# A graph attention layer on one core: edge features loaded a second time in transposed layout, in place of transposes on TensorE and copies on ACT

## The chip, the core and the metric

The kernel runs on one core of one Trainium2 chip. The metric is device time in microseconds (us) of the whole execution; lower is better. A core has TensorE (PE in the profile, with its weight loads as PEld), VectorE (DVE), ScalarE (ACT), GpSimd (POOL) and SyncE (SP), which only issues transfers here. The engines run side by side and wait for each other by semaphores.

## What is computed

One layer of graph attention over 6250 nodes and 206250 edges sorted by target node, then a residual addition. Cut to what matters:

```
h  = relu(layernorm(x))                       # (6250, 256)
xm = h @ W_n2m.T;  xl = xm @ Wl.T + bl;  xr = xm @ Wr.T + br       # (6250, 128)
e  = (edge_attr @ W_r2m.T) @ We.T             # (edges, 128), edge_attr is (206250, 32)
z  = xl[src] + xr[dst] + e
logits = sum over each head's 16 columns of leaky_relu(z, 0.2) * att       # 8 heads
alpha  = softmax of logits over the edges of each dst (own loop edge with the mean attributes added)
out    = segment_sum(xl[src] * alpha, dst) + bias
result = x + out @ W_m2n.T
```

## The kernel before

**Prologue.** The node tables are made: `xl_table` in DRAM (the rows that edges gather), `xr_parts` in SBUF (xr in three bfloat16 parts), `Wc` (the product of the two edge weights; its 32 rows stand four times over the 128 partitions) and `Wc2`, in which each pair of row groups is kept apart from the other by zeros. The list of edges is cut into pieces of 256 edges, and each piece is bound to a window of 128 target nodes.

**Edge loop.** 427 steps (`STEPS`), each of 512 edges: two pieces, h = 0 and 1. Every engine has its own stream of instructions, written by hand, in loops of 48 steps (`UNROLL`); `sweep` gives the step k and its place s in the loop. What an engine does in step k, in this order:

- SP (L748 to L770): for each piece a transfer of edge attributes into `rbf` (a ring of 24 steps, a partition holds two neighbouring edges of each piece), one of the one-hot's slots into `slot_bc` (a ring of 8), and the masks of the running maxima. Ahead of `rbf` it waits until ACT has copied the attributes of step k - 24 (`attr_ready`), ahead of `slot_bc` until VectorE has made the one-hot of step k - 8 (`ohT_ready`). At 16 steps in all it copies a part of x to the output.
- GpSimd (L773 to L780): four gathers of 128 rows each of `xl_table` into `xl_g` (a ring of 24). It waits only for `msg_ready` of step k - 24.
- TensorE: z, transposed (128 features by 256 edges in each of two banks), is summed from three products of `xr_parts` with the one-hot (L794), the edge product `Wc2` by `rbfT` (L800: four matmuls of 128 columns, of which the two pieces use rows 0 to 63 and 64 to 127 of the array), and `xl_g` turned by the identity (L813). Between these last two stands the transpose of the next step's `rbf` (L808) into bank 2. Then come the logits of step k - 1 (L844) and the aggregation of step k - 17 (`LAG`, L860), whose first half's sum, `U_ps[0]`, lies in bank 2 too.
- ACT: distances and one-hots for the aggregation (L898, L903), the copy of the transposed attributes into `rbfT` (L907), the relu of z (L913), and the copy of `rbf` into `msg` (L915).
- VectorE: the addition of the first half's sum to `acc` (L955), the one-hot of step k + 2 (L965), the second half's addition (L979), the messages of step k - 16 (L989, L993), and `uT` of step k (L999), after which z's banks are free for the next step (`u_ready`).

Every 8 steps (`BATCH`) the running maxima of the softmax are brought up to date (L1008 and behind, L825, L833, L870).

**Finale.** Seven batches of node windows: loop edges, shares, projection, addition of x.

Of the kernel before, what the change touches and what calls it, by code (L numbers as in the profile page):

```python
# [36 lines left out]
SRING = 8  # L37
MRING = 3
# [77 lines left out]
def gat_kernel(nc, x, src, dst, edge_attr, W_n2m, W_r2m, Wl, bl, Wr, br, We, att, bias, W_m2n, out):  # L116
# [10 lines left out]
    with ExitStack() as ctx:  # L127
        def sb(name, shape, dt=FP32):
# [11 lines left out]
        Wc2 = sb("Wc2", [P, PT, D_MSG])  # L140
# [6 lines left out]

        banks = ctx.enter_context(nc.psum_tensor("banks", [P, 8, 512], FP32))
# [3 lines left out]
                 xr_parts, ident, ident16, ones, iota_n, node_of, att_bc, att_pad, Wc, Wc2, W_outT,  # L152
                 bias_col, minus_slot, src_tab, win_tab, edge_tab)

        acc = sb("acc", [P, WINDOWS, AGG])
        edge_loop(nc, banks, xl_table, slot_dram, masks_dram, edge_attr,
                  xr_parts, ident, ident16, ones, iota_n, node_of, att_pad, Wc2, minus_slot, src_tab, win_tab,
# [4 lines left out]
def prologue(nc, banks, xl_table, meta_dram, slot_dram, masks_dram, inputs,  # L162
             xr_parts, ident, ident16, ones, iota_n, node_of, att_bc, att_pad, Wc, Wc2, W_outT,
             bias_col, minus_slot, src_tab, win_tab, edge_tab):
# [5 lines left out]
    with ExitStack() as ctx:  # L170
# [3 lines left out]
        def sem(name):  # L174
# [58 lines left out]
        rows_in = [sem(f"rows_in{i}") for i in range(CHUNKS)]  # L233
# [6 lines left out]
        halo_set, head_set, pad_set, att_placed, w2_set, w2_ready = map(  # L240
            sem, ("halo_set", "head_set", "pad_set", "att_placed", "w2_set", "w2_ready"))
# [290 lines left out]
        def _(dve):  # L532
# [118 lines left out]
def edge_loop(nc, banks, xl_table, slot_dram, masks_dram, edge_attr,  # L651
              xr_parts, ident, ident16, ones, iota_n, node_of, att_pad, Wc2, minus_slot, src_tab, win_tab, edge_tab,
# [10 lines left out]
    with ExitStack() as ctx:  # L663
# [11 lines left out]
        rbfT = sb("rbfT", [P, 2, P])  # L675
# [21 lines left out]
        rbfT_ps, LT_ps = banks[:, 2, 0:P], [banks[:, 3 + 3 * par, 0:PIECE] for par in (0, 1)]  # L697
# [679 lines left out]
```

## Time and profile before

| | |
|---|---|
| Time, median of 3 runs | 3654.3 us (3628.19 to 3661.28) |
| Span of the profiled execution, first to last instruction | 2427.2 us |
| Granted TensorE clock, mean | 0.984 |
| Data moved | 244.85 MB, mean 101 GB/s |
| Edge loop in the span | from about 127 to 2337 us |

The profile tells of one execution, from its first to its last instruction. The times come from the whole execution; for the profiled one no total is given beside its span, and what fills the difference to the runs' times isn't in the profile. A row "x1708 | 1637.8, 959 | 522.9 <-issue 515.0" reads: 1708 instructions, engine busy 1637.8 us with them, 959 ns for one, and the engine idle for 522.9 us just before them, 515.0 of it ended by nothing that the profile shows. Matmuls overlap, so the start of the next block tells more than the length of one. An fp32 matmul is recorded as two instructions.

### The profile page before, as it was taken

The page shows a single profiled execution, that of the slowest core. Times are in us where ns is not written, and L with a number is a line of the kernel's source. Part 1 is how long each engine was busy: PE and PEld are TensorE (multiplying, and loading weights), DVE is VectorE, ACT ScalarE, POOL GpSimd, SP SyncE. Part 2 cuts the span into 40 slices and gives each one's busy share as a digit, 9 for nine tenths or more (in the row PEclk, how much of TensorE's full clock was granted, in tenths as well). Part 3 has the DMA queues.
Part 4 walks back from the last instruction along what each step waited for, and adds up shares of the span by engine and source line. Part 5 has one row for each costly group of instructions (what it writes and reads, how often), then busy time and mean ns, then how long its engine had stood idle before and what let it go on. Part 6 is the DMA issues. An engine that isn't in the chain of part 4 may idle for free. (4 is left out here: it accounts for less than half of the span.)

```text
span 2427.2 us, 71208 instructions
## 1 busy us (share of the span) xinstructions
PE 2249.0 (93%) x16556; PEld 1730.1 (71%) x16557; DVE 1481.8 (61%) x4178; ACT 1438.7 (59%) x4332; POOL 1722.3 (71%) x1914
## 2 busy tenths in 40 slices
PE   3968999989999999999999999999999999999977
PEld 2745777767777777777777777777777777777756
DVE  4734656656666666566656665666566656666677
ACT  2714666656665666566656665666566656666653
POOL 3777777777777777777777777777777777777501
PEclk9989999999999999999999999999999999999999
DMA  6244444444444444444444444444444444444117
GB/s 199 80 110 94 103 103 98 97 101 105 99 100 101 106 98 98 101 107 98 98 101 106 98 99 102 106 99 99 101 105 98 99 102 106 98 99 99 47 45 130
DMA packets 288536, 244.85 MB, mean 101 GB/s; under 512 B 168519, under 2 KB 259624, under 8 KB 287842
## 3 DMA queue, kind: packets, MB, share of 16 engines
q1 hardware_dynamic: 221742, 116.00, 21.3%
q0 software_dynamic: 60704, 120.20, 21.2%
q10 hardware_dynamic: 5652, 3.68, 0.5%
q8 instruction: 169, 2.77, 0.5%
q14 instruction: 269, 2.20, 0.3%
HBM read 228.23 MB, written 19.40 MB: 102 GB/s over the span
## 5 line engine op out<-in xcount | busy, mean ns | idle before, releaser
L778 POOL DMA_INDIRECT xl_g<-xl_table,src_tab x1708 | 1637.8, 959 | 522.9 <-issue 515.0
L999 DVE SCALAR_TENSOR_TENSOR uT<-banks,relu 128x256 f32<-128x256 f32 x854 | 347.3, 422 | 544.4 <-issue 517.8
L860 PE MATMUL banks<-msg,onehot 128*128 128x177 f32 x3416 | 632.3, 328 | 7.0 <-DVE acc L955 2.6
L860 PEld LDWEIGHTS banks<-msg,onehot 128*128 128x128 f32 x3416 | 516.8, 191 | 168.8 <-issue 152.3
L898 ACT ACTIVATE distance<-iota_n,minus_slot 128x128 f32<-128x128 f32 x1708 | 541.1, 390 | 0.0
L813 PE MATMUL banks<-ident,xl_g 128*128 128x128 f32 x3416 | 464.2, 280 | 36.2 <-DMA xl_g<-xl_table,src_tab 35.8
L813 PEld LDWEIGHTS banks<-ident,xl_g 128*128 128x128 f32 x3416 | 443.5, 201 | 44.5 <-DMA xl_g<-xl_table,src_tab 43.8
L913 ACT ACTIVATE relu<-banks 128x256 f32<-128x256 f32 x854 | 315.9, 383 | 149.6 <-PE banks L813 116.0
L794 PE MATMUL banks<-onehotT,xr_parts 128*128 128x256 bf16 x2562 | 356.4, 276 | 23.8 <-issue 18.6
L903 ACT ACTIVATE onehot<-distance 128x512 f32<-128x512 f32 x427 | 269.0, 630 | 113.9 <-PE banks L860 101.4
L907 ACT ACTIVATE rbfT<-banks 128x128 f32<-128x128 f32 x427 | 116.5, 273 | 353.5 <-PE banks L808 342.1
L955 DVE TENSOR_TENSOR acc<-acc,banks 128x177 f32 x427 | 145.0, 340 | 285.4 <-PE banks L860 212.3
L800 PE MATMUL banks<-rbfT,Wc 64*128 64x128 f32 x3416 | 310.1, 301 | 0.0
L794 PEld LDWEIGHTS banks<-onehotT,xr_parts 128*128 x2562 | 245.8, 98 | 76.8 <-issue 34.1
L989 DVE TENSOR_TENSOR msg<-xl_g,banks 128x512 f32<-128x512 f32 x427 | 291.1, 682 | 2.8 <-PE banks L871 2.4
L800 PEld LDWEIGHTS banks<-rbfT,Wc 64*128 64x128 f32 x3416 | 227.5, 189 | 90.3 <-issue 88.9
L844 PE MATMUL banks<-uT,att_pad 128*64 128x256 f32 x1708 | 280.8, 408 | 0.0
L808 PE MATMUL banks<-ident,rbf 128*128 128x128 f32 x427 | 141.7, 332 | 42.6 <-DVE acc L955 33.6
L965 DVE TENSOR_SCALAR onehotT<-slot_bc,node_of 128x512 bf16<-128x512 bf16 x427 | 153.1, 359 | 9.9 <-DMA slot_bc<-slot_dram 8.8
L979 DVE TENSOR_TENSOR acc<-acc,banks 128x177 f32 x427 | 144.3, 338 | 12.8 <-PE banks L860 4.9
L844 PEld LDWEIGHTS banks<-uT,att_pad 128*64 128x64 f32 x1708 | 85.1, 136 | 66.0 <-DVE uT L999 25.4
L808 PEld LDWEIGHTS banks<-ident,rbf 128*128 128x128 f32 x427 | 59.7, 140 | 101.5 <-DVE acc L955 46.8
(200 smaller groups left out, 1642.2 us busy)
## 6 DMA issues: line engine op xcount, KB each, us to landing
slot_bc<-slot_dram SPq DMA_DIRECT2D x427, 128.0 KB
xl_g<-xl_table,src_tab POOLq DMA_INDIRECT x1708
rbf<-in_edge_attr SPq DMA_DIRECT2D x854, 32.0 KB
masks<-masks_dram SPq DMA_DIRECT2D x864, 12.1 KB
out<-in_x SPq DMA_DIRECT2D x16, 336.0 KB
out<-result POOLq DMA_DIRECT2D x6, 896.0 KB, 9.5
xl_table<-lr_sb SPq DMA_DIRECT2D x49, 64.0 KB, 1.5
xl_in<-xl_table SPq DMA_DIRECT2D x7, 448.0 KB, 4.7
```

The costliest lines, as they stand in the source:

```text
L778: pool.indirect_dma_start(out=xl_g[:, k % RING, t], out_offset=None, in_=xl_table, in_offset=bass.IndirectOffsetOnAxis(ap=src_tab[:, e:e + ...
L794: nc.tensor.matmul(z_ps[h], parts_of(xr_parts, w[h], part), onehotT[:, n4, h * PIECE:(h + 1) * PIECE], start=part == 0, stop=False)
L800: nc.tensor.matmul(z_ps[h][:, i::PT], Wc2[q, i], rbfT[q, n], start=False, stop=False)
L808: nc.tensor.transpose(rbfT_ps, rbf[:, n], ident[:]).then_inc(rbfT_done, 1)
L813: mm = nc.tensor.matmul(z_ps[h][:, i::PT], xl_g[:, s % RING, i * SPLIT + h], ident[:], start=False, stop=i == PT - 1)
L844: mm = nc.tensor.matmul(LT_ps[par][h * ROWS:(h + 1) * ROWS], att_pad[:, ROWS - HEADS - i * HEADS:2 * ROWS - HEADS - i * HEADS], uT[:, n, h ...
L860: mm = nc.tensor.matmul(U_ps[h], onehot[:, j % 2, t], msg[:, j % 2, t], start=i == 0, stop=i == PT - 1)
L898: nc.scalar.activation(distance[:, t], iota_n[:], ACT.Abs, bias=minus_slot[:, one(TILES * (k - LAG + 1) + t)]).then_inc(dist_ready, 1)
L903: nc.scalar.activation(onehot[:, m % 2], distance[:], ACT.Relu, scale=-1.0, bias=1.0).then_inc(oh_ready, TICK)
L913: nc.scalar.activation(relu[:, h], z_ps[h], ACT.Relu, scale=1.0 - SLOPE).then_inc(relu_ready, 2 + h)
L989: nc.vector.tensor_tensor(to[:, :, :, 0:D_HEAD], xl_g[:, m % RING].rearrange("p t (h d) -> p t h d", d=D_HEAD), w_ps[:, :, row].unsqueeze( ...
L999: nc.vector.scalar_tensor_tensor(out=uT[:, s % 2, h * PIECE:(h + 1) * PIECE], in0=z_ps[h], scalar=SLOPE, in1=relu[:, h], op0=ALU.mult, op1 ...
```

## The change

The host passes a second array, `attr_cols`, which is `edge_attr_32` transposed (32 rows of 206250). SP loads for each piece of a step 32 rows by 256 edges of it into `attrT`, a ring of 4 steps (`TRING`): piece 0 lies in partitions 0 to 31, piece 1 in 32 to 63. TensorE multiplies `Wc` by it with two matmuls of 256 columns. The transposes, bank 2's part for them, ACT's copies, `rbfT` and `Wc2` with its fill and copies go. `rbf` is still loaded, for the copy into `msg`, ahead of which ACT now waits for its transfer. Ahead of a step's first transfer SP waits until TensorE has finished z of step k - 4.

```
@@ edge_loop, sync
-                    for h, e in enumerate(entries(nc, mybir.EngineType.SP, edge_tab, k, E - PIECE)):
+                    edges = entries(nc, mybir.EngineType.SP, edge_tab, k, E - PIECE)
+                    if inside(k - TRING, STEPS):
+                        sp.wait_ge(z_done, Z * (k - TRING + 1))
+                        sp.sem_inc(z_seen, 1)
+                    for h, e in enumerate(edges):
+                        sp.dma_start(attrT[h * D_RBF:(h + 1) * D_RBF, s % TRING], attr_cols[:, bass.DynSlice(e, PIECE)]
+                                     ).then_inc(turned_in[s % TRING], 16)
                         sp.dma_start(rbf[:, s % RING, h * PT * D_RBF:(h + 1) * PT * D_RBF],
...
@@ edge_loop, tensor
-                    pe.wait_ge(rbfT_ready, k + 1)
-                    for i in range(PT):
-                        for h in range(SPLIT):
-                            q = slice(h * PT * D_RBF, (h + 1) * PT * D_RBF)
-                            nc.tensor.matmul(z_ps[h][:, i::PT], Wc2[q, i], rbfT[q, n], start=False, stop=False)
-                if inside(k + 1, STEPS):
-                    n = (s + 1) % RING
-                    pe.wait_ge(loads[n], (r * (UNROLL // RING) + (s + 1) // RING + 1) * FULL)
-                    if inside(k, STEPS):
-                        pe.wait_ge(rbfT_ready, k + 1)
-                    if inside(k - LAG - 1, STEPS):
-                        pe.wait_ge(added, TICK * (k - LAG - 1) + 1)
-                    nc.tensor.transpose(rbfT_ps, rbf[:, n], ident[:]).then_inc(rbfT_done, 1)
-                if inside(k, STEPS):
+                    pe.wait_ge(turned_in[s % TRING], (r * (UNROLL // TRING) + s // TRING + 1) * FULL)
+                    for h in range(SPLIT):
+                        q = slice(h * D_RBF, (h + 1) * D_RBF)
+                        nc.tensor.matmul(z_ps[h], Wc[q], attrT[q, s % TRING], start=False, stop=False)
...
-                        if h == 0 and inside(k + 1, STEPS):
-                            pe.wait_ge(rbfT_ready, k + 2)
@@ edge_loop, scalar
-                if inside(k + 1, STEPS):
-                    act.wait_ge(rbfT_done, k + 2)
-                    nc.scalar.activation(rbfT[:, (s + 1) % 2], rbfT_ps, ACT.Copy).then_inc(rbfT_ready, 1)
...
+                    act.wait_ge(loads[m % RING], (r * (UNROLL // RING) + (s - LAG + 1) // RING + 1) * FULL)
@@ prologue, vector
-            nc.vector.memset(Wc2[:], 0.0).then_inc(w2_set, 1)
-            dve.wait_ge(w2_set, 1)
-            for t in range(TILES):
-                q = slice(t * D_RBF, (t + 1) * D_RBF)
-                nc.vector.tensor_copy(Wc2[q, t % PT], Wc[q, :]).then_inc(w2_ready, 1)
@@ kernel
-        a = np.ascontiguousarray(inputs[name])
+        arrays[f"in_{name}"] = np.ascontiguousarray(inputs[name])
+        if name == "edge_attr_32":
+            arrays["in_attr_cols"] = np.ascontiguousarray(np.asarray(inputs[name]).T)
```

How it stands on TensorE, from the edge product of a step inside the loop to its aggregation, before:

```order
L800 MATMUL banks<-rbfT,Wc 128x128 [waits rbfT_ready]
L800 MATMUL banks<-rbfT,Wc 128x128 x3
L808 MATMUL banks<-ident,rbf 128x128 [waits added,rbfT_ready,loads5]
L813 MATMUL banks<-ident,xl_g 128x128 [waits gathers4]
L813 MATMUL banks<-ident,xl_g 128x128 x3
L844 MATMUL banks<-uT,att_pad 64x256 [waits u_ready]
L844 MATMUL banks<-uT,att_pad 64x256
L860 MATMUL banks<-msg,onehot 128x177 [waits added,oh_ready,rbfT_ready,attr_ready,msg_ready]
```

The same place in the changed kernel, where the lines are L801 (edge product), L805 (xl_g), L825 (a batch's work, which falls on this step), L836 (logits) and L850 (aggregation):

```order
L801 MATMUL banks<-attrT,Wc 128x256 [waits turned_in1]
L801 MATMUL banks<-attrT,Wc 128x256
L805 MATMUL banks<-ident,xl_g 128x128 [waits gathers5]
L805 MATMUL banks<-ident,xl_g 128x128 x3
L825 MATMUL banks<-ones,end_row 128x1 [waits lr_ready]
L825 MATMUL banks<-ones,end_row 128x1
L836 MATMUL banks<-uT,att_pad 64x256 [waits u_ready]
L836 MATMUL banks<-uT,att_pad 64x256
L850 MATMUL banks<-msg,onehot 128x177 [waits oh_ready,added,attr_ready,msg_ready]
```

Two matmuls stand in place of four, the transpose and its waits are gone, and the wait for the attributes is now one for a transfer.

On SP, one step inside the loop, before (L87 reads the pieces' first edges from a table):

```order
L87 ISA [waits attr_ready]
L87 TENSOR_LOAD edge_tab
L752 ISA
L752 DMA rbf<-in_edge_attr 128x64
L752 ISA
L752 DMA rbf<-in_edge_attr 128x64
L756 REGISTER_ALU
L757 ISA [waits ohT_ready]
L757 DMA slot_bc<-slot_dram 128x512
```

And the same step of the changed kernel:

```order
L88 ISA [waits attr_ready]
L88 TENSOR_LOAD edge_tab
L749 ISA
L752 REGISTER_ALU [waits z_done]
L752 DMA attrT<-in_attr_cols 32x256
L754 ISA
L754 DMA rbf<-in_edge_attr 128x64
L752 REGISTER_ALU
L752 DMA attrT<-in_attr_cols 32x256
L754 ISA
L754 DMA rbf<-in_edge_attr 128x64
L758 REGISTER_ALU
```

The transfer of `slot_bc` follows behind these rows as before; ahead of it there are now four transfers in place of two, and the wait for `z_done`.

## Rows read from the trace of the kernel before

**Rows 1.** The page: busy time by engine; SP's DMA queue (packets, MB, share).
```profile
PE 2249.0 (93%) x16556; PEld 1730.1 (71%) x16557; DVE 1481.8 (61%) x4178; ACT 1438.7 (59%) x4332; POOL 1722.3 (71%) x1914
...
q1 hardware_dynamic: 221742, 116.00, 21.3%
```

**Rows 2.** Groups of instructions: the gathers.
```profile
L778 POOL DMA_INDIRECT xl_g<-xl_table,src_tab x1708 | 1637.8, 959 | 522.9 <-issue 515.0 <-DVE msg L989 5.2 <-DVE msg L993 2.7
```

**Rows 3.** The gathers' line: ns min/median/max, first and last start.
```profile
L778 POOL DMA_INDIRECT xl_g<-xl_table,src_tab x1708: 940/944/1910, 127.7 to 2285.0; - x190
```

**Rows 4.** TensorE in order of time, a short step (start us, us).
```profile
1207.14 0.82 PE L794 MATMUL banks<-onehotT,xr_parts 128*128 128x256 bf16 x6
1207.88 0.72 PE L800 MATMUL banks<-rbfT,Wc 64*128 64x128 f32 x8
1208.53 0.33 PE L808 MATMUL banks<-ident,rbf 128*128 128x128 f32 x1
1208.70 1.10 PE L813 MATMUL banks<-ident,xl_g 128*128 128x128 f32 x8
1209.72 0.65 PE L844 MATMUL banks<-uT,att_pad 128*64 128x256 f32 x4
1210.31 1.47 PE L860 MATMUL banks<-msg,onehot 128*128 128x177 f32 x8
1211.61 0.82 PE L794 MATMUL banks<-onehotT,xr_parts 128*128 128x256 bf16 x6
```

**Rows 5.** Who waited for whom: us in total, times, longest us.
```profile
ACT rbfT L907 <- PE banks L808: 342.1, 318, 9.8
...
PEld banks L813 <- DMA xl_g<-xl_table,src_tab: 43.8, 40, 2.9
...
PEld banks L860 <- ACT rbfT L907: 14.2, 37, 0.4
...
DVE onehotT L965 <- DMA slot_bc<-slot_dram: 8.8, 4, 4.3
```

**Rows 6.** The same view of SP's queue.
```profile
SPq L87 <- ACT msg L915: 497.3, 340, 14.6
```

**Rows 7.** TensorE in order of time at the loop's end.
```profile
2288.03 1.16 PE L813 MATMUL banks<-ident,xl_g 128*128 128x128 f32 x8
```

**Rows 8.** The transposes' line: what ended TensorE's idle time before them.
```profile
  DVE acc L955: 80.3, 128
```

**Rows 9.** Prologue in order of time: copies of Wc2, first projection.
```profile
62.43 0.96 DVE L618 COPY Wc<-Wc 32x128 f32<-32x128 f32 x4
...
66.14 0.42 DVE L634 TENSOR_TENSOR lr_sb<-banks,lr_bias 128x256 f32<-128x256 f32 x1 [2.05 <-PE banks L528]
```

**Rows 10.** The loop's first steps in order of time: SP and VectorE.
```profile
127.90 0.90 SPq L752 DMA_DIRECT2D rbf<-in_edge_attr  x2
...
128.85 0.43 SPq L757 DMA_DIRECT2D slot_bc<-slot_dram  x1
...
129.32 0.69 SPq L767 DMA_DIRECT2D masks<-masks_dram  x2
...
130.98 0.92 SPq L752 DMA_DIRECT2D rbf<-in_edge_attr  x2
...
132.59 0.35 DVE L965 TENSOR_SCALAR onehotT<-slot_bc,node_of 128x512 bf16<-128x512 bf16 x1 [4.31 <-DMA slot_bc<-slot_dram]
```

**Rows 11.** SP in order of time, a step inside the loop.
```profile
1216.68 0.91 SPq L752 DMA_DIRECT2D rbf<-in_edge_attr  x2
...
1218.29 0.84 SPq L767 DMA_DIRECT2D masks<-masks_dram  x2
```

**Rows 12.** In order of time: step 209's xl_g product, step 213's one-hot.
```profile
1193.72 1.16 PE L813 MATMUL banks<-ident,xl_g 128*128 128x128 f32 x8 [0.85 <-DMA xl_g<-xl_table,src_tab]
...
1201.12 0.35 DVE L965 TENSOR_SCALAR onehotT<-slot_bc,node_of 128x512 bf16<-128x512 bf16 x1
```

**Rows 13.** The line of the rbf issues: ns min/median/max.
```profile
L752 SPq DMA_DIRECT2D rbf<-in_edge_attr x854: 343/357/1756, 127.9 to 2251.6; - x171
```

More of the change, by code:

```diff
@@ L37 @@
 SRING = 8
+TRING = 4
 MRING = 3
@@ L112, in at, with gat_kernel @@
     return tile[:, bass.DynSlice(w, 1), :].rearrange("p a d -> p (a d)")
-def gat_kernel(nc, x, src, dst, edge_attr, W_n2m, W_r2m, Wl, bl, Wr, br, We, att, bias, W_m2n, out):
+def gat_kernel(nc, x, src, dst, edge_attr, attr_cols, W_n2m, W_r2m, Wl, bl, Wr, br, We, att, bias, W_m2n, out):
     xl_table = nc.dram_tensor("xl_table", (WINDOWS * P + 1, D_MSG), FP32, kind="Internal").ap()
@@ L146, in gat_kernel @@
         edge_tab = sb("edge_tab", [1, WALK], I32)
+        rows_in = [ctx.enter_context(nc.semaphore(f"rows_in{i}")) for i in range(CHUNKS)]
         banks = ctx.enter_context(nc.psum_tensor("banks", [P, 8, 512], FP32))
@@ L162, in prologue @@
 def prologue(nc, banks, xl_table, meta_dram, slot_dram, masks_dram, inputs,
-             xr_parts, ident, ident16, ones, iota_n, node_of, att_bc, att_pad, Wc, Wc2, W_outT,
-             bias_col, minus_slot, src_tab, win_tab, edge_tab):
+             xr_parts, ident, ident16, ones, iota_n, node_of, att_bc, att_pad, Wc, W_outT,
+             bias_col, minus_slot, src_tab, win_tab, edge_tab, rows_in):
     x, src, dst, W_n2m, W_r2m, Wl, bl, Wr, br, We, att, bias, W_m2n = inputs
@@ L648, in _, with edge_loop @@
                     masks_of(masks_b[0:r, c, q], keys[0:r, c, q * PIECE:(q + 1) * PIECE + 2], i + 1)
-def edge_loop(nc, banks, xl_table, slot_dram, masks_dram, edge_attr,
-              xr_parts, ident, ident16, ones, iota_n, node_of, att_pad, Wc2, minus_slot, src_tab, win_tab, edge_tab,
+def edge_loop(nc, banks, xl_table, slot_dram, masks_dram, edge_attr, attr_cols,
+              xr_parts, ident, ident16, ones, iota_n, node_of, att_pad, Wc, minus_slot, src_tab, win_tab, edge_tab,
               acc, x, out):
@@ L674, in edge_loop @@
         onehotT = sb("onehotT", [P, 4, GROUP], BF16)
-        rbfT = sb("rbfT", [P, 2, P])
+        attrT = sb("attrT", [SPLIT * D_RBF, TRING, PIECE])
         relu = sb("relu", [P, SPLIT, PIECE])
@@ L696, in edge_loop @@
         z_ps = [banks[:, h, 0:PIECE] for h in range(SPLIT)]
-        rbfT_ps, LT_ps = banks[:, 2, 0:P], [banks[:, 3 + 3 * par, 0:PIECE] for par in (0, 1)]
+        LT_ps = [banks[:, 3 + 3 * par, 0:PIECE] for par in (0, 1)]
         turned = banks[:, 4].rearrange("p (i c r) -> p i c r", i=2, c=PT)
@@ L706, in edge_loop @@
         slots_in = [sem(f"slots_in{i}") for i in range(SRING)]
+        turned_in = [sem(f"turned_in{i}") for i in range(TRING)]
         gathers = [sem(f"gathers{i}") for i in range(RING)]
         masks_in = [sem(f"masks_in{i}") for i in range(MRING)]
+        z_seen = sem("z_seen")
         FULL, GATHERED = SPLIT * 16, TILES * 16
-        (set_up, acc_zero, ohT_ready, node_saved, rbfT_done, rbfT_ready, z_done, relu_ready, u_ready, L_done, dist_ready, oh_ready,
+        (set_up, acc_zero, ohT_ready, node_saved, z_done, relu_ready, u_ready, L_done, dist_ready, oh_ready,
          attr_ready, msg_ready, agg_done, added, forth_done, run_done, ends_done, seq_ready, seq_half, seq_done,
@@ L713, in edge_loop @@
          last_ready, weight_ready, wT_done, spread_done, factor_ready, rescaled, x_set) = map(sem, (
-             "set_up", "acc_zero", "ohT_ready", "node_saved", "rbfT_done", "rbfT_ready", "z_done", "relu_ready", "u_ready", "L_done",
+             "set_up", "acc_zero", "ohT_ready", "node_saved", "z_done", "relu_ready", "u_ready", "L_done",
              "dist_ready", "oh_ready", "attr_ready", "msg_ready", "agg_done", "added", "forth_done", "run_done",
```

19 lines of the change are left out of this document (8 added, 11 removed).

## The prediction

> **What bounds the kernel now.** I read the page's engine shares and slices first. TensorE is busy for 93% of the span and GpSimd for 71%, at a granted clock of 0.984 (the table), so TensorE looks like the bound [rows 1]. The reader is to see next, by the groups, that GpSimd's idle time isn't slack: 1708 gathers of xl_g, and before 1682 of them GpSimd sat idle for 515.0 us with no releaser, 0.306 us each time [rows 2]. A gap of one size before nearly every gather, ended by nobody, is part of issuing the next one. GpSimd thus runs gathers back to back from the first at 127.7 to the last at 2285.0 us, (2285.0 - 127.7) / 1707 = 1.264 us each and 5.055 us for the four of a step [rows 3]. 427 steps at 5.055 us are 2158 us, the whole edge loop. What stands before it (127.7) and behind the last gather (2427.2 - 2285.9 = 141.3) makes up the rest of the 2427.2 us.
>
> TensorE's own short step is 4.47 us (from the one-hot block at 1207.14 to that at 1211.61), 0.59 under GpSimd's pace [rows 4]; the steps that carry a batch's work use that up. It still waits 43.8 us in 40 places for a gather's landing [rows 5], and at the loop's end the last product with xl_g starts at 2288.03, 2.1 us behind the last gather's end: TensorE is pinned to GpSimd to the end [rows 3, 7]. So two engines are nearly level, and **GpSimd's gathers set the pace**.
>
> **The change part by part.** The sum is made on the profiled span, 2427.2 us; the median of the timed runs is 3654.3 us. The 1227.1 us between them stand in no row, and I carry them over unchanged (this is my weakest step, see the rivals). A page of the Trainium skill, Runtime: NRT & Kernel Launch, section The ~15µs preamble/postamble breakdown, puts what surrounds a kernel at 9 to 15 us; the measured difference here is eighty times that, the measurement decides, and what it consists of no row here shows. By the page the total would be some 2440 us and the change's share of it larger; nothing below uses that.
>
> *TensorE's transposes* go: 427 blocks of 0.17 us (1208.53 to 1208.70) = 73 us [rows 4]. With them go their waits for the accumulator addition, 80.3 us in 128 places, since the transposes shared a bank with the sum of the first half, and 14.2 us in which the aggregation waited for ACT's copy [rows 5, 8]. Some of these 80.3 us will come back as the aggregation's own wait for the same addition, which starts 1.8 us later (1208.53, 1210.31) [rows 4].
>
> *The product with the edge weights* keeps its columns: 4 matmuls of 128 columns become 2 of 256. The block takes 0.65 us now (1207.88 to 1208.53). The nearest row with 256 columns whose two halves of the array run at once is the logit block: 0.59 us (1209.72 to 1210.31) [rows 4]. I take 0.59, -0.06 us or -26 us in all. No row shows tiles of 32 rows side by side. If they ran one behind the other, the block would cost like 8 unpaired instructions of the xl_g block, 1.02 us (1208.70 to 1209.72), +0.37 us or +158 us [rows 4]. The other end of the bound is 0.59. The Trainium skill, TensorE: Matmul & The Clock Gate, section Measured speedup vs the span model, has 32-row tiles in distinct row groups running together (3.07 times for four tiles), which speaks for the low end.
>
> TensorE is thus relieved of 73 + 26 + up to 94 = 99 to 193 us, 0.23 to 0.45 us a step. **None of it lies on the path**, because a gather still comes every 1.264 us. The gain turns into longer waits of the xl_g product for its gather.
>
> *ACT's copies* go, one a step, and 342.1 us of waiting for the transposes [rows 5]. Its relu follows the xl_g product as before. Gain on the path: nothing. The added wait for `loads` before its copy into msg concerns a transfer issued 16 steps ago: nothing.
>
> *The prologue* loses the fill of Wc2 and four copies, which take 0.96 us together. VectorE afterwards sits idle for 2.05 us until the first projection, so this is hidden; bounds 0 and, with as much as one copy for the fill, -1.2 us, I take 0 [rows 9].
>
> *SP's queue* is where the change can cost. It issues two more transfers a step, 854 of 32 KB. One more in a row costs 0.54 us (two rbf issues take 0.90 from start to end, one 0.36). SP's free-running step is 3.08 us (127.90 to 130.98), the registers of the loop add 0.3 (from the rbf issue at 1216.68 to the end of masks at 1219.13 are 2.45 us against 2.11 from 127.90 to 130.01) [rows 10, 11, 13], so the new step is 3.08 + 0.34 + 1.08 + some 0.1 for the new wait and count = 4.6 us. That is under 5.055, with 0.45 us left: hidden as long as an issue doesn't get dearer.
>
> And SP now waits. Until now it waited 497.3 us for ACT's copy of 24 steps before [rows 6], and for slot_bc for a one-hot of 8 steps before. Now each step waits until z of 4 steps before is done (`z_done`), and behind this wait stand rbf, slot_bc and masks of the same step. attrT itself has 3 steps, over 13 us, to land: enough. slot_bc has less: VectorE builds step k's one-hot 2 steps ahead, and uT of step k-2 is queued behind it on VectorE, which TensorE's next step waits for. From the end of z of step k-4 to that one-hot are 6.2 us (the xl_g block from 1193.72 ends at 1194.88, the one-hot starts at 1201.12) [rows 12], the tightest place that I found in that stretch. The new slot_bc needs 4 issues of 0.54 ahead of it, 2.2 us, and then 3.7 us from its issue to its first reader (128.85 to 132.59) [rows 10], 5.9 together. With 0.2 us less in TensorE's step some 0.1 us of slack is left, in one step of eight. Late once a batch by 0.5 us, that is 54 x 0.5 = 27 us of VectorE's time, which the 0.23 to 0.45 us a step that TensorE gained (1.8 us a batch at least) absorb. I take 0; bounds 0 and +27 us.
>
> *The DMA engines* carry 26 MB more. Gathers of 0.94 us run up to 1.91, and all together lose 1708 x (0.959 - 0.944) = 26 us in this way, and the issues on SP stretch likewise [rows 2, 3, 13]. The hardware queue grows from 116 to 142 MB, by 23% [rows 1]. I take 26 x 0.23 = +6 us; bounds -10 us (the transfers come more evenly spaced) and +26.
>
> **Sum:** 0 (TensorE, ACT) + 0 (prologue) + 0 (slot_bc) + 6 = +6 us. The span becomes 2433 us and the time 3654.3 + 6 = **3660 us**: no change. What moves the time by less than 1% (37 us) a measurement of this kernel can't tell from no change.
>
> **The rivals.** *TensorE was the bound after all* (in the timed runs at least). 3654.3 / 2427.2 is 1.51, and a TensorE at the lower of its two levels, 1.2 in place of 2.4 GHz, would give such a factor. Its step would then be up to twice 4.47 us, well over GpSimd's 5.055, and the cut would be worth between 427 x 0.17 = 73 and, with everything at half speed and the shorter product, 427 x 2 x 0.23 = 196 us; I take 125: 3530 us. For it: the missing 1227 us and their size. Against: the profile's clock, 0.98.
>
> *SP becomes the bound* (slower than before). It decides from 0.45 us more per step: if an attrT issue costs 0.8 us in place of 0.54, or slot_bc lands 1 us later throughout, a step takes 5.2 us, and 427 x 0.15 = 64 us come on top: 3724 us. For it: single issues of rbf have taken up to 1.76 us. Against: their median, 0.357 [rows 13].
>
> *The unpaired product* (32-row tiles one behind the other) costs TensorE 158 - 73 = +85 us against slack of 44 plus up to 94: between 0 and +41 us, 3654 to 3701.
>
> *The time outside the rows grows with the tensors.* The program's inputs and its output have 41 MB, the added copy 26.4: 1227 x 26.4 / 41 = +790 us, 4450. Nothing in the profile speaks for it but that the gap is large.
>
> **How the numbers follow.** No change (GpSimd's pace): 0.62. TensorE as the bound: 0.14. SP as the bound: 0.12. The unpaired product: 0.03, half of it within 1%. Copying outside: 0.05. Shifts of 1 to 1.5% by the DMA engines, either way: 0.02 and 0.02. Faster by over 1% is then 0.14 + 0.02 = 0.16, slower 0.12 + 0.015 + 0.05 + 0.02 = 0.20, same 0.64. The range goes from 3530 (the faster rival, so that less than 0.2 is left out) to 3735; of the likeliest case alone it is 3635 to 3690.
>
> **What the profile of the changed kernel would show.** GpSimd: 1708 gathers at 1.26 us, 2158 us from first to last. TensorE: its share falls from 93% to about 87%, the wait of the xl_g product for gathers rises from some 44 us to 150 or more. The product with Wc has a block of 0.59 us; 1.0 us means unpaired tiles. VectorE's waits for slot_bc, 8.8 us now [rows 5], stay under 50 us; hundreds of us there mean SP's rival. SP's wait moves from ACT's copy to the xl_g product. A span that falls by 100 us refutes the gathers as the bound; a span that stands while the time moves refutes the constant remainder.

## The result: 3.8% faster, outside the range

Before 3653.8 us (3628.2 to 3661.3, 4 runs), after **3508.4 us** (3485.4 to 3537.6, 4 runs), ratio **0.9624** with a 95% interval of [0.9563, 0.9685]. Forecast were 3660 us and 3530 to 3735.

One fact has to come first, since no number below can be read without it: a chip is in one of two conditions, which changed between comparisons and not within one. In the one, called quiet here, the kernel before takes 2426 us; in the other, called disturbed as in the expectations, 3640 to 3700 us (medians). The comparisons ran on five chips, but the condition isn't a matter of the chip: one and the same chip was quiet for the first comparison below and disturbed for the second, ten minutes later. (One of the 46 runs of before beside the experiments fits neither: 6961 us, among quiet ones.) The four timed runs of each kernel were disturbed; the execution whose rows the prediction rests on was quiet. In both conditions a run's time is its span plus some 2 us (3485.44 against 3483.5, 2425.01 against 2423.2). So next to nothing lies outside the span: the 1227 us that I carried over as a remainder are inside the loop. (The Trainium skill, Runtime: NRT & Kernel Launch, section The ~15µs preamble/postamble breakdown, has 9 to 15 us around a kernel; the measured difference here is 2, and the measurement decides.)

The page of the kernel after, disturbed, answers to [rows 1]:

```profile
span 3483.5 us, 69178 instructions
...
PE 2667.9 (77%) x14421; PEld 1834.2 (53%) x14422; DVE 1476.6 (42%) x4173; ACT 1323.8 (38%) x3905; POOL 1713.0 (49%) x1914
...
PEclk9758878877888888889787778888789887888899
...
q1 hardware_dynamic: 262734, 144.04, 18.9%
```

GpSimd is busy for 1713.0 us as before, but that is now 49% of the span. The gathers' line, which answers to [rows 2, 3], shows that they no longer set the pace: a gather still takes 0.95 us, yet GpSimd waits 1106.3 us for VectorE's msg, that is for a free buffer of xl_g, 24 steps behind.

```profile
L780 POOL DMA_INDIRECT xl_g<-xl_table,src_tab x1708: 942/947/1400, 127.3 to 3314.2; - x190
its engine sat idle before it (us, times) until:
  DVE msg L981: 1106.3, 303
```

Who waited for whom in it (us in total, times, longest us), beside [rows 5]:

```profile
ACT relu L900 <- remote: 863.1, 191, 37.4
DVE uT L987 <- issue: 856.2, 334, 47.8
...
DVE onehotT L953 <- DMA slot_bc<-slot_dram: 438.0, 169, 6.6
PE banks L796 <- DVE uT L987: 400.1, 159, 9.6
```

"Remote" is a wait at whose end no instruction of another engine has just finished. What has come just then is the signal itself, the semaphore's update. ACT stands ready for z, 191 times, when z has been made already. A place of the same kind, in order of time (the wait's own record is missing, so the row says "issue"; the trace has an update of `z_done`, TensorE's signal for z, at 1815.93):

```profile
1807.77 1.16 PE L805 MATMUL banks<-ident,xl_g 128*128 128x128 f32 x8
...
1809.44 1.47 PE L850 MATMUL banks<-msg,onehot 128*128 128x177 f32 x8
...
1810.17 0.37 ACT L900 ACTIVATE relu<-banks 128x256 f32<-128x256 f32 x1
1810.23 0.69 SPq L754 DMA_DIRECT2D rbf<-in_edge_attr  x1
...
1811.62 0.50 PE L796 MATMUL banks<-onehotT,xr_parts 128*128 128x256 bf16 x3
...
1813.07 0.71 SPq L759 DMA_DIRECT2D slot_bc<-slot_dram  x1
...
1816.01 0.39 ACT L900 ACTIVATE relu<-banks 128x256 f32<-128x256 f32 x1 [5.47 <-issue]
...
1816.49 0.42 DVE L987 SCALAR_TENSOR_TENSOR uT<-banks,relu 128x256 f32<-128x256 f32 x1 [5.44 <-issue]
...
1817.06 0.82 PE L796 MATMUL banks<-onehotT,xr_parts 128*128 128x256 bf16 x3 [4.93 <-DVE uT L987]
```

TensorE ends both halves of z at 1808.93. ACT takes the first at 1810.17 and the second at 1816.01, with 5.47 us of idle time ahead of it; VectorE's uT and then TensorE's next step follow at once. Meanwhile SyncE's issues come 2.8 us apart (1810.23, 1813.07, then masks at 1815.92; from the rbf issues to masks it was 1.6 us [rows 11]). The windows around this place (length, busy us of each engine, then TensorE's granted clock) show a second cost:

```profile
1810.00:1816.00 6.00, 2.13 (x16) 1.69 (x14) 0.42 (x1) 0.53 (x2) 4.50 (x5) 1.00 0.45 87
...
1818.00:1820.00 2.00, 2.00 (x9) 1.35 (x10) 1.29 (x5) 1.92 (x6) 0.44 (x1) 0.50 0.09 20
1820.00:1822.00 2.00, 2.00 (x9) 1.04 (x8) 0.81 (x2) 1.29 (x6) 1.45 (x2) 0.50 0.39 101
...
1824.00:1826.00 2.00, 2.00 (x16) 1.41 (x15) 1.00 (x4) 0.63 (x1) 0.26 (x1) 1.00 0.11 33
```

While it stands idle for 4.93 us TensorE falls to the lower of its levels (0.50, 1.2 GHz), has it until about 1823, and its blocks take longer: the product with Wc that starts at 1817.81 takes 1.23 us in place of 0.70. GpSimd goes on gathering through the stall.

### The profile page after: what moved, and what is told of

Its sections match the earlier page's. It is cut to its first block and busy times, and to the rows that moved or that the text cites. A ratio compares the mean times of both kernels' runs of the same rounds, so it can differ in the third digit from the quotient of the medians.

```text
span 3483.5 us, 69178 instructions
## 1 busy us (share of the span) xinstructions
PE 2667.9 (77%) x14421; PEld 1834.2 (53%) x14422; DVE 1476.6 (42%) x4173; ACT 1323.8 (38%) x3905; POOL 1713.0 (49%) x1914
## 3 DMA queue, kind: packets, MB, share of 16 engines
q1 hardware_dynamic: 262734, 144.04, 18.9%
## 5 line engine op out<-in xcount | busy, mean ns | idle before, releaser
L780 POOL DMA_INDIRECT xl_g<-xl_table,src_tab x1708 | 1628.2, 953 | 1562.1 <-DVE msg L981 1106.3
L796 PE MATMUL banks<-onehotT,xr_parts 128*128 128x256 bf16 x2562 | 458.2, 314 | 638.4 <-DVE uT L987 400.1
L850 PE MATMUL banks<-msg,onehot 128*128 128x177 f32 x3416 | 735.2, 359 | 105.0 <-DVE acc L967 77.3
L850 PEld LDWEIGHTS banks<-msg,onehot 128*128 128x128 f32 x3416 | 588.9, 213 | 335.9 <-issue 223.5
L805 PEld LDWEIGHTS banks<-ident,xl_g 128*128 128x128 f32 x3416 | 520.7, 233 | 181.6 <-issue 181.6
L805 PE MATMUL banks<-ident,xl_g 128*128 128x128 f32 x3416 | 616.1, 335 | 0.1
L801 PE MATMUL banks<-attrT,Wc 32*128 32x256 f32 x1708 | 364.0, 508 | 0.0
L836 PE MATMUL banks<-uT,att_pad 128*64 128x256 f32 x1708 | 340.1, 482 | 2.7 <-issue 2.7
L801 PEld LDWEIGHTS banks<-attrT,Wc 32*128 32x128 f32 x1708 | 152.8, 218 | 102.3 <-issue 87.5
L836 PEld LDWEIGHTS banks<-uT,att_pad 128*64 128x64 f32 x1708 | 97.7, 156 | 81.7 <-issue 51.3
L903 ACT ACTIVATE msg<-rbf 128x128 f32<-128x128 f32 x427 | 130.7, 306 | 0.1
L981 DVE COPY msg<-banks 128x64 f32<-128x64 f32 x427 | 95.8, 224 | 0.0
```

Source lines behind the costliest of these rows:

```text
L780: pool.indirect_dma_start(out=xl_g[:, k % RING, t], out_offset=None, in_=xl_table, in_offset=bass.IndirectOffsetOnAxis(ap=src_tab[:, e:e + ...
L796: nc.tensor.matmul(z_ps[h], parts_of(xr_parts, w[h], part), onehotT[:, n4, h * PIECE:(h + 1) * PIECE], start=part == 0, stop=False)
L801: nc.tensor.matmul(z_ps[h], Wc[q], attrT[q, s % TRING], start=False, stop=False)
L805: mm = nc.tensor.matmul(z_ps[h][:, i::PT], xl_g[:, s % RING, i * SPLIT + h], ident[:], start=False, stop=i == PT - 1)
L836: mm = nc.tensor.matmul(LT_ps[par][h * ROWS:(h + 1) * ROWS], att_pad[:, ROWS - HEADS - i * HEADS:2 * ROWS - HEADS - i * HEADS], uT[:, n, h ...
L850: mm = nc.tensor.matmul(U_ps[h], onehot[:, j % 2, t], msg[:, j % 2, t], start=i == 0, stop=i == PT - 1)
```

## The experiments

Ratios are to the kernel before on the same chip in the same comparison; "TensorE idle" is counted in the profiled run's trace: the gaps of over 1.5 us between its matmuls, from the first gather to the last.

**What the change is worth on the quiet chip.** One run of each kernel; before ran beside them in 2427.2 us.

`b_again` is the kernel before, `after_again` the kernel after, `tring8` the kernel after with

```
-TRING = 4
+TRING = 8
```

> The kernel before, unchanged, for a second profile: the first one's span is 2427 us while its runs took about 3650, and in the changed kernel span and time differ by 2 us. Theory 1 (the profiled execution was an undisturbed one, the timed ones were stalled inside the span): time about 3650, span about 3648, TensorE's granted clock about 0.8, and between the steps stalls of several us such as the changed kernel shows in ACT's wait for z or SP's issues. Theory 2 (a constant lies outside the span): span 2427 again and the time 1227 above it.

> The changed kernel unchanged, for a second profile. 3508 us, span about 3506, clock 0.82 and the same stalls, if its first profile is typical. If spans like 2427 us appear in one execution of several whatever the kernel, this one may show it: then about 2430.

> The changed kernel with a ring of 8 steps for attrT in place of 4, so that SP may run 8 steps ahead of z. In the changed kernel's profile VectorE waits 438 us for slot_bc. Theory A (SP's wait for z of 4 steps before makes slot_bc late and this costs time): the wait falls under 100 us and the time from 3508 to 3100 to 3300. Theory B (stalls in which SP and ACT are both slow set the pace, slot_bc is a victim): the wait shrinks but the time stays within 3450 to 3550.

Measured: 2425.0, 2430.3 and 2421.7 us. All three are within 0.25% of 2427: here the forecast of no change holds. The page of after_again, its gathers' line, its last product with xl_g, and then its waits:

```profile
PE 2254.0 (93%) x14421; PEld 1615.7 (67%) x14422; DVE 1460.3 (60%) x4173; ACT 1340.1 (55%) x3905; POOL 1715.6 (71%) x1914
...
L780 POOL DMA_INDIRECT xl_g<-xl_table,src_tab x1708: 940/944/1397, 125.7 to 2276.4; - x190
...
2291.04 1.16 PE L805 MATMUL banks<-ident,xl_g 128*128 128x128 f32 x8
```

```profile
POOL xl_g L780 <- issue: 509.5, 1664, 2.5
DVE onehotT L953 <- DMA slot_bc<-slot_dram: 472.7, 285, 6.8
...
PEld banks L805 <- DMA xl_g<-xl_table,src_tab: 44.9, 52, 3.1
...
PE banks L805 <- DMA xl_g<-xl_table,src_tab: 24.8, 29, 2.7
```

slot_bc is late in 285 steps, 472.7 us, where I had set 50 as the bound, and TensorE's gain of slack is eaten by it: its waits for gathers stand at 44.9 + 24.8 us and not at 150. More than that: the last product with xl_g starts 13.6 us behind the last gather's end (2291.04 against 2277.4), where in before it was 2.1 [rows 3, 7]. TensorE has fallen behind the gathers, which a ring of 24 steps allows, and the loop ends by that much later. The gathers themselves ran 5.3 us shorter than in b_again (1.260 us each against 1.263). With eight buffers (tring8, the same view) SyncE isn't held to TensorE's z so closely:

```profile
PEld banks L805 <- DMA xl_g<-xl_table,src_tab: 158.7, 176, 2.8
PE banks L805 <- DMA xl_g<-xl_table,src_tab: 89.9, 103, 2.4
DVE onehotT L953 <- DMA slot_bc<-slot_dram: 38.7, 18, 4.9
```

That is the picture which I had predicted for the change itself, and the time is still that of the gathers: its last product starts 2.0 us behind the last of them.

**With one gather of four left out.** `b_g3` and `a_g3` are before and after with

```
-                for t in range(TILES):
+                for t in range(TILES - 1):
```

so GpSimd needs 3.8 us a step. The fourth slice of xl_g is zeroed once, and the output isn't the layer's.

> The kernel before with three gathers a step in place of four (the fourth tile of xl_g is filled with zeros once, so the output isn't the layer's). Theory 1 (undisturbed, the gathers' 1.264 us set the pace and TensorE stands some 0.1 us a step behind): GpSimd needs 3.79 us a step, TensorE becomes the bound with its 4.9 to 5.0, and the span falls only to 2360 to 2410 us. Theory 2 (something disturbs the loop, as in the 3650 us runs): about 3600, the gathers don't matter.

> The changed kernel with the same three gathers a step and the same omission. Theory 1 (the change relieves TensorE by 0.2 to 0.45 us a step, which the fourth gather covers): 100 to 190 us under the run above, 2180 to 2300. Rival (SP's wait for z of 4 steps before makes slot_bc late, and this eats the gain as soon as the gathers no longer cover it): within 40 us of the run above.

Measured: 3088.9 and 2929.5 us, with before beside them at 3692.5: the disturbed condition, which showed me that it was there. The change gives 5.2% (one run each); the 159 us lie in the 100 to 190 that I had expected, but that was for the other condition and another reason. A gather less gives 16% although GpSimd was busy for under half of the span, which the gathers' issue as a bound doesn't explain, and both of my theories of b_g3 missed it. The waits of b_g3 pointed to what does differ between the kernels:

```profile
ACT rbfT L907 <- remote: 629.1, 106, 11.6
PEld banks L860 <- ACT rbfT L907: 434.2, 128, 5.3
```

**The kernel before, disturbed, and three edits of the kernel after.** `b_again2` is before. `a_round` puts the transpose, ACT's copy and both waits for it back (the product still reads attrT):

```
+                    nc.tensor.transpose(rbfT_ps, rbf[:, n], ident[:]).then_inc(rbfT_done, 1)
...
+                        if h == 0 and inside(k + 1, STEPS):
+                            pe.wait_ge(rbfT_ready, k + 2)
...
+                    act.wait_ge(rbfT_done, k + 2)
+                    nc.scalar.activation(rbfT[:, (s + 1) % 2], rbfT_ps, ACT.Copy).then_inc(rbfT_ready, 1)
```

`a_turn` puts the first of these lines back alone, without its signal (with the transpose's own waits, for its operand and its bank). `a_dve` takes ACT out of the way from z to uT:

```
-                        nc.scalar.activation(relu[:, h], z_ps[h], ACT.Relu, scale=1.0 - SLOPE).then_inc(relu_ready, 2 + h)
...
+                        nc.vector.tensor_scalar(relu[:, h], z_ps[h], SLOPE, None, ALU.mult).then_inc(relu_ready, 2 + h)
```

> The kernel before, unchanged, to have its trace beside the next three. If the chip is in the condition of the first three experiments: 2425 us, gathers back to back at about 5.05 us a step. If it is in that of the timed runs: 3650 to 3690 us, the clock near 0.82 to 0.9, and then the round-trip theory wants the aggregation's wait on TensorE for ACT's copy into rbfT (14.2 us where nothing is disturbed) to be hundreds of us, as with three gathers (391.5 and 434.2 us); the TensorE-work theory wants TensorE busy throughout, with no such wait among its largest.

> The kernel after, with TensorE's transpose of the edge features, ACT's copy of it into rbfT and the aggregation's wait for that copy put back; the product still reads attrT, so the copies feed nothing. It holds the round trip alone. Undisturbed: 2425 to 2435 us by every theory. Disturbed: the round-trip theory expects the time of before, 3620 to 3690 us, with the aggregation waiting hundreds of us for the copy. The theory that it is TensorE's work expects the same as a_turn within 1%. The theory that the four paired products are what was gained (8 small ones before) expects 3510 us, the time of after.

> The kernel after, with TensorE's transpose alone put back, its result read by nobody and waited for by nobody. Undisturbed: 2425 to 2435 us. Disturbed: the round-trip theory expects the time of after, 3490 to 3540 us; the TensorE-work theory expects at least half of the way back to before, 3580 us or more.

> The kernel after, with ACT's relu of z taken out: VectorE makes 0.2 z and then the larger of it and z, so the way from TensorE's z to uT no longer passes ACT; VectorE has two more operations a step over 256 columns each, about 0.7 to 0.9 us in all. Undisturbed: 2425 to 2440 us, unless VectorE comes to set the step. Disturbed: if signals between engines that arrive late are what makes the time, one hand-over fewer in each step gains as the change did, 3350 to 3450 us; if busy time makes it, VectorE's 0.8 us a step more gives nothing or costs up to 340 us, 3510 to 3850 us.

| disturbed, before 3702.5 us | us | ratio | 95% |
|---|---|---|---|
| b_again2 | 3703.5 | 0.9999 | [0.9975, 1.0023] |
| a_round | 3667.5 | 0.9902 | [0.9873, 0.9931] |
| a_turn | 3571.9 | 0.9644 | [0.9525, 0.9763] |
| a_dve | 3571.0 | 0.9641 | [0.9582, 0.9701] |

The three edited kernels ran twice each. In us a_turn lies outside what I wrote for the round-trip theory; before was slower here than in the timed runs, so the ratio is to be read.

The trace of before in this condition (b_again2) has the place that the quiet one hid. Its page and its waits:

```profile
PE 2541.0 (69%) x16556; PEld 1948.3 (53%) x16557; DVE 1486.6 (40%) x4178; ACT 1414.0 (38%) x4332; POOL 1706.6 (46%) x1914
```

```profile
ACT rbfT L907 <- remote: 1041.1, 136, 41.7
PEld banks L860 <- ACT rbfT L907: 826.1, 167, 7.9
PE banks L860 <- ACT rbfT L907: 782.0, 173, 7.4
```

The 14.2 us of [rows 5] have become some 800. One of them in order of time:

```profile
1509.18 0.33 PE L808 MATMUL banks<-ident,rbf 128*128 128x128 f32 x1
1509.35 1.06 PE L813 MATMUL banks<-ident,xl_g 128*128 128x128 f32 x8
1510.33 0.65 PE L844 MATMUL banks<-uT,att_pad 128*64 128x256 f32 x4
...
1517.62 0.28 ACT L907 ACTIVATE rbfT<-banks 128x128 f32<-128x128 f32 x1 [8.71 <-remote]
1517.80 0.66 ACT L913 ACTIVATE relu<-banks 128x256 f32<-128x256 f32 x2
1517.95 2.73 PE L860 MATMUL banks<-msg,onehot 128*128 128x177 f32 x8 [6.97 <-ACT rbfT L907]
```

The transpose ends by 1509.51. ACT copies it at 1517.62. It isn't ACT that is slow: the trace has the update of `rbfT_done`, TensorE's signal, at 1517.60, and in the 136 places of the first line above ACT starts within 0.03 us of the update. The signal comes 8 us late. The aggregation, whose operands are all there, stands from 1510.98 to 1517.95, because its bank is the one that ACT still has to read; then it runs at the lower clock (2.73 us against 1.47). In the kernel after, a signal that is late in the same way lets TensorE do the aggregation and stops it only in the next step (1811.62 to 1817.06 above).

How large the two costs are, for before: from quiet (b_again) to disturbed (b_again2) its span grows by 1285 us. TensorE's gaps of over 1.5 us grow by 951 of them, from 32 us (14 gaps) to 983 (192), and the lower clock stands for some 1160 us of the span in place of 85 (twice the missing share of the mean granted clock, 0.844 against 0.983). In the kernel after the gaps are 622 us (141) and the mean clock is 0.825: 361 us of idle time fewer, of which the span keeps 225. That the lower clock takes the rest is likely, not shown.

So the theory of a round trip stands, and that of TensorE's work falls: the transposes alone cost nothing that can be told (0.9644 against 0.9624, with an interval of 1.2% either way), the round trip takes back 2.6%. a_dve was to show whether every hand-over fewer gains, and I had expected 3350 to 3450 us if so: without ACT's relu it stays where after is. That speaks against this wider form, but doesn't refute it, since VectorE is busy for 279 us more (1755.9 us against 1476.6), which may hide a gain. There ACT's lateness goes to its next wait on TensorE (onehot, 525.9 us "remote"), and TensorE's wait for uT grows to 665.7 us.

**Work or hand-over?** `a_copy` has the transpose and a copy of equal size on ACT, from SBUF, and no waits between them; `a_tiny` is a_round with one column copied (167 ns on ACT in place of 273, so a good part of ACT's work remains); `tring8_b` is tring8; `after_again2` is after.

```
# a_copy
+                    nc.scalar.activation(rbfT[:, (s + 1) % 2], rbf[:, (s + 1) % RING], ACT.Copy).then_inc(rbfT_ready, 1)
# a_tiny, against a_round
-                    nc.scalar.activation(rbfT[:, (s + 1) % 2], rbfT_ps, ACT.Copy).then_inc(rbfT_ready, 1)
+                    nc.scalar.activation(rbfT[:, (s + 1) % 2, 0:1], rbfT_ps[:, 0:1], ACT.Copy).then_inc(rbfT_ready, 1)
```

> The kernel after, unchanged, beside the next three. Disturbed (before beside it near 3700 us): 0.962 of before, 3540 to 3580 us, so the lone transposes measured earlier (0.9644 of before) cost nothing that can be told. Undisturbed: 2430 us.

> The kernel after with the transpose put back and read by nobody, and with a copy of the same size put back on ACT at its old place, which reads the edge features in SBUF and is waited for by nobody: TensorE's work and ACT's work of the old way without the hand-over between them. Disturbed: if the hand-over is the price, as after, 0.96 to 0.97 of before (3550 to 3590 us); if ACT's 0.3 us a step is, as the full round trip, 0.985 to 0.995 (3645 to 3680 us). Undisturbed: 2425 to 2435 us.

> The kernel after with the whole round trip put back, but ACT copies one column of the 128: the hand-over and both waits without ACT's work. Disturbed: if the hand-over is the price, 0.985 to 0.995 of before (3645 to 3680 us), with the aggregation waiting hundreds of us for the copy; if ACT's work is, 0.96 to 0.97. Undisturbed: 2425 to 2435 us.

> The kernel after with eight buffers of attrT in place of four, so that SyncE may run eight steps ahead and not four. Disturbed: VectorE's waits for slot_bc (438 us in the profiled run of after, up to 6.6 us each) should go, and if they are on the path, the time falls by 50 to 200 us, to 3360 to 3520 us; if they lie in the shadow of ACT's late relu, it stays within 1% of after. Undisturbed: 2422 us as measured before.

**Which half of it?** `a_to_act` adds to a_copy that ACT's copy waits for the transpose (which then gives its signal), `a_to_pe` that the aggregation waits for ACT's copy. `a_eight` has the product in four matmuls of 128 columns, as before; the eight are its records. `a_rows4` loads 4 rows of attrT's 32, so z lacks 28 of the 32 features. `a_to_act2` is a_to_act once more.

```
# a_to_act, against a_copy
+                    act.wait_ge(rbfT_done, k + 2)
# a_to_pe, against a_copy
+                            pe.wait_ge(rbfT_ready, k + 2)
# a_eight, against after
+                        for i in range(PT):
+                            nc.tensor.matmul(z_ps[h][:, i::PT], Wc[q], attrT[q, s % TRING, i::PT], start=False, stop=False)
# a_rows4, against after
-                        sp.dma_start(attrT[h * D_RBF:(h + 1) * D_RBF, s % TRING], attr_cols[:, bass.DynSlice(e, PIECE)]
+                        sp.dma_start(attrT[h * D_RBF:h * D_RBF + 4, s % TRING], attr_cols[0:4, bass.DynSlice(e, PIECE)]
```

> The one without hand-over (transpose and a copy of SBUF put back), with ACT's copy now waiting for the transpose, and TensorE still waiting for nothing of it: the hand-over from TensorE to ACT alone. Disturbed: a signal that reaches ACT late also holds up the relu queued behind it; if this half is the price, 0.98 to 0.99 of before; if the other half is, 0.96 to 0.967. Undisturbed: 2425 to 2435 us.

> The same kernel without hand-over, with the aggregation waiting for ACT's copy of SBUF, and ACT waiting for no transpose: the hand-over from ACT back to TensorE alone. The copy stands ahead of the relu, before which ACT has waited for nothing of TensorE's but the aggregation of 17 steps ago, so it should be made long before the aggregation. Disturbed: 0.96 to 0.97 of before if that is so, 0.98 to 0.99 if the way back is what costs. Undisturbed: 2425 to 2435 us.

> The kernel after with the product of the edge features in eight matmuls of 128 columns each, as before, in place of two of 256... the strided columns of attrT against the same strided columns of z. It looks for the third of the gain that the round trip does not account for (before against the full round trip put back: 1%). Disturbed: 0.97 to 0.975 of before if the number of instructions of the product is that third, 0.96 to 0.965 if it is not. Undisturbed: 2425 to 2435 us.

> The kernel after, but each load of attrT brings 4 rows of the 32, the others are zeroed once: an eighth of the second load's packets and bytes, the same instructions, signals and waits. The result lacks 28 of 32 edge features in z. Disturbed: if the traffic of the second load costs there, this gains on after by up to the 5 to 6% that one gather in four gave per byte, 3350 to 3450 us; if not, within 1% of after. Undisturbed: 2422 to 2432 us.

> The hand-over from TensorE to ACT alone, as in a_to_act, once more, since that comparison fell in the undisturbed condition (before at 2426 us), where it shows nothing of the disturbed one. Disturbed (before near 3650 to 3700 us): 0.98 to 0.99 of before if the price is ACT standing in its queue for TensorE's signal, 0.96 to 0.967 if it is TensorE standing for ACT's copy, since TensorE waits for nothing here. Undisturbed: 2442 us again.

| disturbed | before us | us | ratio | 95% | TensorE idle us (gaps) |
|---|---|---|---|---|---|
| after_again2 | 3644.0 | 3500.0 | 0.9605 | not given | 612 (146) |
| a_copy: work, no hand-over | 3644.0 | 3516.8 | 0.9655 | [0.9598, 0.9711] | 704 (141) |
| a_to_act2: and TensorE to ACT | 3642.2 | 3543.0 | 0.9729 | [0.9682, 0.9777] | 668 (141) |
| a_tiny: both waits, less work | 3644.0 | 3604.4 | 0.9882 | [0.9846, 0.9917] | 733 (175) |
| tring8_b | 3644.0 | 3523.5 | 0.9647 | [0.9555, 0.9739] | 746 (144) |

a_round has 847 us in 186 gaps, b_again2 983 in 192. The ratio of after_again2 is that of the medians; its four runs spread from 3463 to 3534 us, and the lower two alone give 0.953. Work on both engines thus costs between nothing and 1.2% (a_copy against 0.9624, 0.9605 and 0.953). ACT's standing for the transpose adds 0.7% (the intervals overlap; 0.9729 lies in neither of the ranges that I had set for the two halves). From there to both waits it is another 1.5%, which the intervals do part, although a_tiny has less of ACT's work: TensorE's standing for ACT's copy is the largest single piece. It is had by subtraction, between two chips; a_to_pe, which has it alone, met the quiet chip, and ACT's copy reads SBUF in a_to_act2 and PSUM in a_tiny, which I didn't separate. The waits in a_tiny, where the copy is one column wide:

```profile
ACT rbfT L910 <- remote: 648.7, 106, 9.2
...
PEld banks L863 <- ACT rbfT L910: 421.1, 96, 7.2
PE banks L863 <- ACT rbfT L910: 381.4, 96, 6.8
```

In a_to_act2 ACT's copy is late nearly as often, and TensorE doesn't stand for it:

```profile
ACT rbfT L908 <- remote: 573.2, 99, 40.9
```

tring8_b is not faster than after: slot_bc's lateness lies in the shadow of the late signals. Of the last 1%, between a_round and before, I know no cause; a_eight was meant for it, but its comparison fell on the quiet chip.

On the quiet chip (before 2425.9 us) a_to_act took 2442.0 us (1.0072, [1.0050, 1.0094]), a_to_pe 2447.2 (1.0086, [1.0068, 1.0104]), a_eight 2446.1 (1.0078, [1.0060, 1.0096]) and a_rows4 2424.4 (0.9989, [0.9979, 0.9999]). The first three miss my 2425 to 2435. Their gathers still take 2156 to 2157 us from first to last, as in before, but the last product with xl_g starts 18.5, 24.8 and 27.5 us behind the last gather (13.6 in after, 1.8 in b_again): TensorE, held up by slot_bc and given back some work, falls further behind, and that is the 0.7 to 0.9%. The kernel after itself, in one run beside before, was at 1.0013 on the quiet chip. a_rows4 has all instructions and waits of after and an eighth of the second load's bytes, and is level with before, with slot_bc late in 56 steps. tring8 has all of the traffic, and slot_bc is late in 18. So it takes both, the traffic and the ring of four steps that holds SyncE back, to make slot_bc late in 285. The waits of a_rows4 have the 150 and more us that I wanted of the change:

```profile
PEld banks L806 <- DMA xl_g<-xl_table,src_tab: 176.2, 206, 2.6
...
PE banks L806 <- DMA xl_g<-xl_table,src_tab: 97.0, 120, 2.2
...
DVE onehotT L955 <- DMA slot_bc<-slot_dram: 65.6, 56, 6.7
```

No version with the right output beats the kernel after in the disturbed condition; tring8, 0.2% under before on the quiet chip in one run, can't be told from it in either.

## Why the prediction was wrong

- **The step that failed** is "the 1227.1 us between them stand in no row, and I carry them over unchanged". They were the same loop in another condition, at 8.0 us a step in place of 5.05 (the gathers of b_again2 run from 124.8 to 3532.4 us; in the kernel after 7.5 us a step). With it fell "the gathers set the pace" for the runs that were timed, and with that the term "none of it lies on the path". The sum +6 us was made for a condition in which it holds.
- **ACT's copies, "Gain on the path: nothing"**, and "14.2 us in which the aggregation waited": on the quiet chip right, in the timed runs the main term. Of the 145 us, the two waits account for some six tenths (0.9655 to 0.9882 is 2.3 of 3.8%). An estimate, made when the result was known: the signal was late 136 times in before, and each time the kernel after has the aggregation, 1.3 us [rows 4], to do meanwhile: 177 us, against 145 measured. Of the other four tenths, some 1% lies between a_round and before without a cause that I know.
- **The rival "TensorE was the bound after all (in the timed runs at least)"** gave 3530 us and the right sign for the wrong reason. The mean clock was 0.82 to 0.84, at the lower level for about a third of the span and not throughout, TensorE was idle for 31% of before's span, and its transposes put back cost nothing that can be told.
- **SP as the bound** didn't come about, but its mechanism did: slot_bc was late in 285 steps and not in one of eight. I had worked its landing time from a first step with an empty queue [rows 10]. The +27 us of my bound were 473 us of waits, not quite absorbed: TensorE's end moved 11.8 us further behind the gathers.
- **The term of +6 us for the DMA engines** had the wrong sign: beside 28 MB more (116.00 to 144.04 MB, not 26) the gathers ran 5.3 us shorter, which is within my bound of -10. That the quiet span went from 2423.2 to 2428.4 us, +5 against my +6, is luck: -5.3 for the gathers, +11.8 for the late end, and the rest; 6 us is also the spread of before's quiet runs (2422.9 to 2429.1).
- **The product**: 0.63 us a block on the quiet chip (1202.32 to 1202.95) against 0.59 forecast and 0.65 before; the halves run paired, and the rival of unpaired tiles is out. TensorE's short step fell from 4.47 to 4.35 us (1201.57 to 1205.92), not to 4.24. Its share stayed at 93% where I said 87%. For a part of that the slack went to waiting for slot_bc through the one-hot, and the records of a block that waits inside still count as busy; but in a_rows4, where slot_bc is seldom late, it is still 91%. 0.12 us a step are 51 us of busy time, which gives some 91%; 87% is had only if the waits that go are taken off too, and these were never busy time.
- **Copying outside the span**: refuted, since only some 2 us are outside.
- **Range**: its low end rested on the rival with TensorE as the bound. I had named the missing 1227 us as the weakest step, and then gave it a chance of 0.19 in all; a time half as long again as the span asked for a wide range on the fast side.

The block rows of after on the quiet chip, which answer to [rows 4]:

```profile
1201.57 0.82 PE L796 MATMUL banks<-onehotT,xr_parts 128*128 128x256 bf16 x6
1202.32 0.70 PE L801 MATMUL banks<-attrT,Wc 32*128 32x256 f32 x4
1202.95 1.16 PE L805 MATMUL banks<-ident,xl_g 128*128 128x128 f32 x8
1204.03 0.65 PE L836 MATMUL banks<-uT,att_pad 128*64 128x256 f32 x4
1204.62 1.47 PE L850 MATMUL banks<-msg,onehot 128*128 128x177 f32 x8
1205.92 0.82 PE L796 MATMUL banks<-onehotT,xr_parts 128*128 128x256 bf16 x6
```

## What to carry to other kernels

When the timed runs and the profiled span differ by more than a few us, the profile is of another condition than the runs: settle that first, and hold the sum back until it is. A wait that costs 14 us in a profile can be the dearest in another condition: count the round trips in which an engine with work in hand stands for a small job of another, because a slack of 0.6 us a step doesn't cover a hand-over that comes 7 us late. In a loop with deep rings compare also where the consumer's last step stands behind the producer's: in the quiet runs the pace of the gathers never changed, and nearly all of the 0.7 to 0.9% came behind the last of them. And a wait that exists only because two tiles share a bank of PSUM puts one engine's lateness into another's queue; the kernel before with the transpose in a bank of its own wasn't tried.

## What I had not expected of the hardware

- The two conditions themselves: 2426 and 3640 to 3700 us for one kernel, both on one chip within ten minutes (2427.2 and 3692.5), and steady within a comparison. In the disturbed one, instructions of SyncE's sequencer that otherwise take 30 to 60 ns take some 700 ns at times: of its some 7000 MOVE, ALU and register instructions none over 500 ns in the quiet trace of after, 737 in the disturbed one. Gathers take 0.95 us in both.
- A signal can come 8 us behind the end of the matmul that gives it (1517.60 against 1509.51), while the engine that waits for it starts 0.02 us after it. On the quiet chip ACT's copies never wait for more than 1 us behind the transpose's end; in b_again2 they do so 136 times.
- The traces of the disturbed condition lack records: of the 427 signals that VectorE's one-hot gives, the trace of before has 410 on the quiet chip and 286 in b_again2. The Trainium skill, NOTIFIC — the notification-queue block, section 7.1 (Overflow: three behaviours, one of which stalls the engine), has a full queue of records either drop a record or hold up the engine that makes it, by how the queue is set. The one would fit lost records and the other late signals, but not both on one queue; no run here tests it, and what disturbs the chip stays open.
- Taking one gather in four away gave 604 us in the disturbed condition, 1.4 us a step, while GpSimd was idle for half the time. Why is open too.
- TensorE's clock fell to 0.50 in an idle stretch of 4.9 us and came back some 6 us after its work had begun again, so a late signal of this length is paid for twice.
